# A graph attention layer and a two-of-eight expert layer on one core: where the routing weights come from, and where ScalarE makes the residual rows

## The reference

```python
x = x + gnn(layernorm(x))            # gnn: attention over the edges, then
                                     # (out - mean) * rsqrt(var + eps) * gamma + beta, mean and var over the nodes,
                                     # and + its own input (the residual)
x = x + ffn(layernorm(x))

# in ffn, for the rows xt of its input:
logits  = xt @ Wr + br
probs   = softmax(logits)
top_p, top_idx = top_k(probs, 2)
weights = top_p / top_p.sum(-1)      # of the two chosen experts
xn      = (xt - mean) * rsqrt(var + eps)
out     = sum over the two of  weight * (gelu((xn * ln_g + ln_b) @ W1 + b1) @ W2 + b2)
```

## Time and profile before

| | |
|---|---|
| median of three executions | 1970.54 us |
| the profiled execution's own time | 1971.19 us |
| its span, which all stretches below count | 1969.4 us |
| PE busy / granted clock over the span | 88% / 0.94 |
| DVE, ACT, POOL busy | 73%, 55%, 62% |
| share of PE, DVE and POOL in the chain that ended last | 49%, 16%, 14% |

### The profile page before, as it was taken

How to read it: one execution, slowest core, us unless ns; L and a number is a source line. 1 busy time by engine, 2 the same in 40 slices (tenths; PEclk the granted TensorE clock), 3 DMA queues, 4 the chain that set the end, 5 groups by cost and what they waited for, 6 DMA issues and landing times.

```text
span 1969.4 us, 36324 instructions
## 1 busy us (share of the span) xinstructions
PE 1734.1 (88%) x10852; PEld 1222.6 (62%) x10852; DVE 1438.8 (73%) x3115; ACT 1080.1 (55%) x2380; POOL 1219.4 (62%) x1150
## 2 busy tenths in 40 slices
PE   7769899999999989989898987644999999999997
PEld 5535555555555545555455554543889898989996
DVE  7777777868788777787877878798666666666664
ACT  5656666656666665666666663662444434343443
POOL 1277777777777777777777774102366565556553
PEclk9979999989999999999999989775999999999999
DMA  5554446455465455654546452387132333333322
GB/s 169 167 151 129 136 140 164 129 142 157 138 167 142 134 147 140 165 141 134 148 139 165 121 136 65 117 290 208 31 53 47 53 47 53 48 52 49 51 42 34
DMA packets 142680, 233.52 MB, mean 119 GB/s; under 512 B 31127, under 2 KB 107553, under 8 KB 141313
## 3 DMA queue, kind: packets, MB, share of 16 engines
q0 software_dynamic: 62800, 147.54, 31.4%
q1 hardware_dynamic: 69765, 81.13, 13.5%
q10 hardware_dynamic: 9932, 2.52, 0.7%
HBM read 188.81 MB, written 43.15 MB: 118 GB/s over the span
## 4 chain that ended last, share of the span: by engine, by line
PE 49%; DVE 16%; POOL 14%; issue 10%; DMA 7%; ACT 2%; DVEq 1%; ACTq 0%; POOLq 0%; SPq 0%
PE bank L1940 14%; POOL gather_ring L1061 14%; PE bank L1957 14%; PE bank L1185 8%; PE bank L1150 6%; DVE acc L1079 4%; DMA gather_ring<-node_table,src_slot 3%; DVE gather_ring L1106 2%; DMA w_stage<-in_L_ffn_W 2%; PE bank L930 2%; PE bank L1161 1%; PE bank L1921 1%; PE bank L678 1%; DVE w_lo L953 1%; ACT r_ring L1330 1%
## 5 line engine op out<-in xcount | busy, mean ns | idle before, releaser
L1061 POOL DMA_INDIRECT gather_ring<-node_table,src_slot x879 | 846.0, 962 | 268.0 <-issue 254.3
L1185 PE MATMUL bank<-gather_ring,onehot 128*128 128x264 f32 x1758 | 479.0, 409 | 91.4 <-DVE acc L1079 87.6
L1079 DVE TENSOR_TENSOR acc<-acc,bank 128x264 f32 x879 | 377.2, 429 | 194.6 <-DVE acc L1079 103.4
L1185 PEld LDWEIGHTS bank<-gather_ring,onehot 128*128 128x128 f32 x1758 | 315.8, 192 | 242.0 <-DVE acc L1079 189.8
L1150 PE MATMUL bank<-ones 128*128 128x512 bf16 x1760 | 421.9, 395 | 0.0
L2024 POOL DMA_INDIRECT out_rows<-y,token_idx x105 | 201.4, 1918 | 221.7 <-DMA out_rows<-y,token_idx 151.1
L1150 PEld LDWEIGHTS bank<-ones 128*128 128x128 bf16 x1760 | 170.3, 101 | 200.8 <-issue 32.6
L1992 ACT ACTIVATE hid<-bank,cols 128x256 f32<-128x256 f32 (+1 forms) x448 | 210.3, 551 | 141.5 <-PE bank L1940 138.6
L1940 PE MATMUL bank<-xe,w_hi 128*128 128x256 f16 (+1 forms) x1792 | 284.7, 267 | 0.9 <-ACT hid L1992 0.5
L1957 PE MATMUL bank<-w,hid_hi 128*128 x1680 | 278.3, 273 | 0.1
L1206 ACT ACTIVATE onehot<-iota_free,neg_dst 128x128 f32<-128x128 f32 x880 | 267.3, 386 | 0.0
(11 more groups left out here) (286 smaller groups left out, 2023.3 us busy)
## 6 DMA issues: line engine op xcount, KB each, us to landing
w_stage<-in_L_ffn_W SPq DMA_DIRECT2D x16, 1024.0 KB, 5.5
dst_row<-dst_rows SPq DMA_DIRECT2D x110, 128.0 KB
gather_ring<-node_table,src_slot POOLq DMA_INDIRECT x879, 2.8
w_split<-w_out SPq DMA_DIRECT2D x32, 256.0 KB, 3.0
w<-w_split SPq DMA_DIRECT2D x8, 1024.0 KB, 13.0
node_table<-acc SPq DMA_DIRECT2D x24, 264.0 KB
xt<-in_x SPq DMA_DIRECT2D x24, 256.0 KB, 3.0
r_ring<-in_x SPq DMA_DIRECT2D x6, 896.0 KB, 10.6
```

Of the source, the lines that this page charges most:

```text
L1061: e.indirect_dma_start(out=gather_ring[:, b % GB, j, :], out_offset=None, in_=node_table, in_offset=bass.IndirectOffsetOnAxis(ap=src_slot[ ...
L1079: e.tensor_tensor(a, a, bank[AGG[s % len(AGG)]][:, 0:ROW].rearrange("p (a c) -> p a c", a=1), ALU.add).then_inc(added, 1)
L1185: e.matmul(bank[AGG[s % len(AGG)]][:, 0:ROW], onehot[:, b % OHB, j, :], gather_ring[:, b % GB, j, :], start=True, stop=True).then_inc(summ ...
```

## The change

In the norm, ACT takes a root of ones first of all, makes the copies of all chunks without residual rows between them, and makes all 24 residual rows behind the root of the variance. In stage 3 the two additions and multiplications of all logits that stood at the head of the routing move into the waits for the roots of the second half, the softmax is gone, the two largest are found among the logits themselves, and ACT takes exp of one number per token, their difference, behind its first two groups of rows. FAR_BELOW is -1e38. At the head of the experts' stage DVE splits the first input before vector_columns and columns, and PE turns the first tiles before it waits for the experts.

```diff
--- before.py
+++ after.py
@@ -1418,14 +1418,12 @@
                                  chunk_bank(c, k)[:, 0:len(at) * P].rearrange("p (n m) -> p n m", m=P), ACT.Copy
                                  ).then_inc(chunk_kept, 1)
 
+            e.activation(sd_col, ones[:, 0:KD], ACT.Sqrt)
             for c in range(CHUNKS):
                 keep(c)
-                for n in range(2 * (c - 2), 2 * (c - 1)):
-                    if 0 <= n:
-                        scalar_resid(e, n)
             e.wait_ge(var_known, 1)
             e.activation(sd_col, var_col, ACT.Sqrt, bias=eps[:, :]).then_inc(sd_made, 1)
-            for n in range(2 * (CHUNKS - 2), RESID_AHEAD):
+            for n in range(RESID_AHEAD):
                 scalar_resid(e, n)
 
         def pool_iotas(e):
@@ -1523,7 +1521,13 @@
                 if n == 6 * NG:
                     gains(0)
             variances(1)
+            pr = prob[:, :, :]
+            e.wait_ge(logits_kept, NT)
+            vector_order.of(e.tensor_tensor(pr, pr, logits[:, :, :], ALU.add))
             second(1)
+            e.wait_ge(vector_order.sem, vector_order.n)
+            vector_order.of(e.tensor_tensor(pr, pr, rs1[:, :].rearrange("p (n a) -> p n a", a=1).broadcast_to([P, NT, NE]),
+                                            ALU.mult))
             gains(1)
 
         def vector_route(e):
@@ -1543,20 +1547,13 @@
             pr, IE = prob[:, :, :], iota_e[:, :, :]
             peak, at, w0, w1 = (top[:, i, :] for i in range(4))
             by_tile = "p n e -> p e n"
-            e.wait_ge(logits_kept, NT)
             e.wait_ge(vector_order.sem, vector_order.n)
-            tt(pr, pr, logits[:, :, :], ALU.add)
-            tt(pr, pr, per_tile(rs1[:, :]), ALU.mult)
             tt(pr, pr, per_expert(br_row[:, :]), ALU.add)
-            reduce_e(peak, pr, ALU.max)
-            e.tensor_tensor(pr, pr, per_tile(peak), ALU.subtract).then_inc(logits_shifted, 1)
-            e.wait_ge(exps_made, 1)
-            reduce_e(peak, pr, ALU.add)
-            chain(e, e.reciprocal(peak, peak))
-            tt(pr, pr, per_tile(peak), ALU.mult)
             for c, best in enumerate((w0, w1)):
                 F3 = first[:, c, :, :]
                 reduce_e(best, pr, ALU.max)
+                if c:
+                    e.tensor_tensor(peak, w1, w0, ALU.subtract).then_inc(logits_shifted, 1)
                 tt(Q, pr, per_tile(best), ALU.is_equal)
                 tt(Q, Q, IE, ALU.mult)
                 reduce_e(at, Q, ALU.min)
@@ -1565,14 +1562,15 @@
                         meta[:, :, FIRST_COL - D:FIRST_COL - D + 1].rearrange("p n a -> p (n a)"), at, float(NE), ALU.add))
                 tt(F3, IE, per_tile(at), ALU.is_equal)
                 if c == 0:
-                    chain(e, e.scalar_tensor_tensor(pr, F3, -2.0, pr, ALU.mult, ALU.add))
+                    chain(e, e.scalar_tensor_tensor(pr, F3, FAR_BELOW, pr, ALU.mult, ALU.add))
             tt(chosen[:, :, :], first[:, 0, :, :], first[:, 1, :, :], ALU.add)
             e.tensor_tensor(chosen[:, :, :], chosen[:, :, :], per_tile(valid[:, :]), ALU.mult).then_inc(chosen_made, 1)
 
-            tt(peak, w0, w1, ALU.add)
-            chain(e, e.reciprocal(peak, peak))
-            vector_order.of(e.tensor_tensor(meta[:, :, 0:1].rearrange("p n a -> p (n a)"), w0, peak, ALU.mult))
-            e.tensor_tensor(meta[:, :, 1:2].rearrange("p n a -> p (n a)"), w1, peak, ALU.mult).then_inc(meta_made, 1)
+            e.wait_ge(exps_made, 1)
+            chain(e, e.tensor_single_scalar(w0, peak, 1.0, ALU.add))
+            chain(e, e.reciprocal(w1, w0))
+            vector_order.of(e.tensor_copy(meta[:, :, 0:1].rearrange("p n a -> p (n a)"), w1))
+            e.tensor_tensor(meta[:, :, 1:2].rearrange("p n a -> p (n a)"), peak, w1, ALU.mult).then_inc(meta_made, 1)
 
             def by_expert(psum):
                 return bank[psum][:, 0:NT * NE].rearrange("p (e n) -> p n e", n=NT)
@@ -1670,7 +1668,6 @@
             tt(slot_e[:, 0, :], slot_e[:, 0, :], slot_e[:, 1, :], ALU.add)
             chain(e, e.tensor_single_scalar(expert_of_slot_f[:, :], slot_e[:, 0, :], float(LAST_E), ALU.min))
             e.tensor_copy(expert_of_slot[:, :], expert_of_slot_f[:, :]).then_inc(experts_known, 1)
-            vector_columns(e)
 
         def tensor_stage3(e):
             e.wait_ge(chunk_kept, KD * CHUNKS)
@@ -1726,16 +1723,18 @@
                                         scale=gain[:, n:n + 1])
                 made.then_inc(rows_made, 1)
 
-            assert GROUPS == RB + 2 and RESID_AHEAD + LATE_AT > RB * NG > 2 * (CHUNKS - 2)
+            assert GROUPS == RB + 2 and RESID_AHEAD + LATE_AT > RB * NG
             for g in range(5):
                 keep_logits(g)
             sds(0)
             keep_logits(5)
             keep_logits(6)
             sds(1)
+            for g in range(2):
+                rows(g)
             e.wait_ge(logits_shifted, 1)
-            e.activation(prob[:, :, :], prob[:, :, :], ACT.Exp).then_inc(exps_made, 1)
-            for g in range(GROUPS):
+            e.activation(top[:, 0, :], top[:, 0, :], ACT.Exp).then_inc(exps_made, 1)
+            for g in range(2, GROUPS):
                 rows(g)
             e.wait_ge(meta_made, 1)
             e.dma_start(x_rows[0:(NT - 1) * P, D:XROW].rearrange("(n p) c -> p n c", p=P), meta[:, 0:NT - 1, :]
@@ -1895,9 +1894,11 @@
             e.wait_ge(experts_known, 1)
             for i in range(2):
                 e.wait_ge(rows_stored[i], (STORED[0], ROWS_STORED)[i])
+            split_input(0)
+            vector_columns(e)
+            e.wait_ge(vector_order.sem, vector_order.n)
             for s in range(2):
                 columns(s)
-            split_input(0)
             for s in range(FS + 1):
                 if s + 1 < FS:
                     split_input(s + 1)
@@ -1959,8 +1960,10 @@
                                             start=(c == 0 and n == 0), stop=(c == KH - 1 and n == 2))
                 made.then_inc(y_done, 1)
 
+            for i in range(2):
+                e.wait_ge(rows_stored[i], (STORED[0], ROWS_STORED)[i])
+            turn(0)
             e.wait_ge(experts_known, 1)
-            turn(0)
             for s in range(FS + 1):
                 if s + 1 < FS:
                     turn(s + 1)
```

## The result

After, the kernel takes **1964.62 us** (median of ten executions, 1962.73 to 1967.84), against 1971.48 for the kernel before on the same chip (ten, 1967.12 to 1975.20). The ratio is 0.9967 with an interval of 0.9958 to 0.9976: 6.5 us faster, between 4.7 and 8.3. I had forecast 10.6 less, 1960.0 within 1957.5 to 1964.2. The direction was right, the size was not. (A ratio here is taken over the executions of both kernels and is not exactly the quotient of the two medians, which differ by 6.9 us.)

The account below looks back on a forecast made before the run. The prediction saw the kernel bound by the engine-to-engine path from the last edge to the first hidden matmul, with DMA transfers beside it. Savings of 6.0 + 4.45 + 0.15 = 10.6 us gave 1960.0, range 1957.5 to 1964.2.

Parts of the forecast that it names:

- The wait for the root: Norm: DVE no longer waits for ACT's root behind the variance; 3.1 us saved.
- the late logits: Start of x1: ACT copies tile 0's logits at 1266.7, not 1264.3; cost nothing, up to 1 us if PE were fast.
- The pace: Norm: without residual rows between the copies DVE sets the pace, its statistics ending 2.9 us earlier.
- loses 1.0 there, once: Norm: DVE waits 1.0 us at chunk 3, because the root and table load delay ACT's first copy.
- The table load: Norm: taken as 1.28 us; by the skill's 2.66 the norm's loss would be 2.4 and the sum 9.2.
- The routing: Stage 3: softmax operations gone, additions and products moved into waits; 4.45 us saved, bounds 4.0 and 4.65.
- Part 3: Experts' head: gathers wait for meta, starting 2.4 us earlier; the fourth tile lands faster, keeping almost all of 4.45.
- The head: Experts' head: splitting the first input ahead of the columns gains at most 0.16 us; 0.15 taken.
- meta holds the experts' start: Rival: meta doesn't move, gathers start at 1363.5 or later; 6.2 to 8.5 saved, 1962.0 to 1964.4; chance 0.24.
- an early rise of the clock: Rival, x1: PE's clock already up for the first tiles, another 2 us gone, 1958.0; chance 0.08.
- a lasting low one: Rival, x1: PE's clock stays down, 0.47 us more per tile; with 40 tiles 18.8 lost, 1978.8; chance 0.03.

Follow-up runs that it names:

- e8: Changed kernel with meta's large store issued behind the fourth group of rows instead of the last; 2312.20 us, ratio 0.9979 to the kernel before.
- e1: Changed kernel, but SP waits for the store of meta before issuing the four late loads of second weights; 1964.37 us, ratio 0.9956 to the kernel before.
- e2: Changed kernel with the root of ones and its table load ahead of ACT's wait for the edges; 1963.38 us, ratio 0.9942 to the kernel before.
- e12: Changed kernel with the edits of e8 and e2, and b2_all loaded by ACT behind the first slot's gelus; 1957.65 us, ratio 0.9921 to the kernel before.
- e6: e1 with the load of b2_all moved behind ACT's copy of the second slot's rows; 2313.72 us, ratio 0.9968 to the kernel before.
- e10: Changed kernel with the experts' head as before: vector_columns and columns ahead of the first split; 1963.84 us, ratio 0.9956 to the kernel before.
- e7: e6 with the late weight loads waiting for the fourth tile instead of meta; 2312.72 us, ratio 0.9981 to the kernel before.
- e9: Changed kernel with the edits of e7 and e2 together; 2305.21 us, ratio 0.9962 to the kernel before.
- e11: Changed kernel with the edits of e8 and e2, and b2_all loaded by SP behind the fourth tile's landing; 1960.79 us, ratio 0.9938 to the kernel before.
- e4: Changed kernel with the norm of the kernel before; 1971.24 us, ratio 0.9984 to the kernel before.

## Why the prediction was wrong

**The norm: right in its mechanism.** The wait for the root was worth 3.20 (predicted 3.1) and the late logits nothing (x1 starts as long behind the reciprocal as before). The pace gave 2.26 instead of 2.9. The step "loses 1.0 there, once" was right for the load itself: with the clock up DVE waits 0.99 once, and a is 15.88 (e8), where my terms sum to 16.0. It rested on PE at 1.15 per chunk, which is PE at the full clock; in after the clock fell for some 3 us behind PE's wait, and a is 16.74. That term I had at nothing. It varies from run to run: with the load in the norm a is 15.88 (e8) to 17.78 (e1), and with the load moved away 14.79 (e2) to 15.80 (e12). What decides whether the clock falls, no run shows; the wait alone does not, since it stayed up in e8 and fell in e12.

**The table load** is 1.28 in the norm (1241.94), and the root of ones starts at 1243.24, 0.02 behind it; at 1316.10 the same 1.28, with exp 0.02 behind. The Trainium skill (ScalarE: Activation LUTs, What ACT_TABLE_LOAD costs) adds about 1.38 for a drain; no such time passes around these two. The loss of nearly 2 in the norm comes close to the 2.4 that I worked out by that figure, but only 1.1 of it is the load, as e8 shows, and the rest is PE's clock.

**The routing: right.** 4.54 in place of 4.45.

**Part 3 failed**, in one sentence: "so I take off what they idled, about 0.8 (bounds nothing and 2.5): meta is there at about 1362.7". Measured by the first matmul of x1, meta landed 1.8 later, outside both bounds. I took the landing as the old one less some idle time of the engines, as if meta moved with its issue. But its last packets get through only when the late weights do, in the kernel before as in after: they ended 0.65 and 0.95 behind the weights' last packet, and with the weights held back (e1) meta landed 12 us earlier. What remained to be counted was packets and not bytes: meta is 0.1 MB, but 6250 packets; beside the rows it moved about one for each of theirs, and what was left moved 8 to 13 in a microsecond beside the 8 KB packets. Why the weights themselves ended 1.2 later in after, counted from x1, and 0.1 to 2.4 later over the four kernels with the new routing and this order, is not shown. In numbers, the first gather was to come 2.4 earlier than before and came 0.8 later by x1's clock (5.15 lost behind token_idx against 4.54 - 0.17 + 0.02 won ahead of it). The other half of part 3 was right: the fourth tile lost its 5.2 and took 2.9, because b2_all was out of the way; e6 against e1 shows it by itself. From token_idx to the first hidden matmul the path lost 2.45, of which I had forecast nothing.

**The head: under-counted**, 0.37 for my "at most 0.16": I had set turn(1)'s end as the bound, and in the earlier trace rows those ends are modelled; hidden(0) starts 0.88 behind turn(1)'s start in after, not 1.09.

**The sum.** 10.6 predicted, 8.1 in the path: -0.64 pace, +0.10 root, -0.17 x1, +0.09 routing, +0.02 list, -2.60 from token_idx to the first hidden matmul, +0.68 experts. The last of these is within what the same code does: over the kernels without the late gelu j goes from 592.1 (e10) to 593.7 (e8). The rival "meta holds the experts' start" had the right mechanism, with 1962.0 to 1964.4 against 1964.62. Its account of the fourth tile was wrong, its bound on meta ("doesn't move at all") too mild. That its upper end came so near the time is partly luck: the fourth tile's 2.3, which it did not have, is set off by the norm's 0.6 and the first gather's 0.8, which it did not have either. That rival had 0.24 from me, on the argument that ACT issues earlier; the earlier issue bought nothing. Of the other rivals, x1 showed neither an early rise of the clock nor a lasting low one: it took 40.38 for 40.21.

**What stays open**: why ACT sees the first hidden half 2 us late when it has just issued b2_all (e6, e7, e9; not in e11, where SP issues it, nor in e12, where ACT does so behind the gelus; both differ in the early store of meta as well); what makes PE's clock fall; and what became of the difference between the path's 8.1 and the whole time's 6.5. Larger pieces for meta, which would cut its packets, were not tried.

## What to carry to other kernels

Where two DMA queues are busy, count packets and not bytes: in this kernel a store in pieces of 16 bytes advanced by about one piece for each 1 KB packet of the other queue, and its last pieces landed when that queue's run of large packets was over. So issue such a store where the other queue's packets are small, or where it is empty, and ask what comes behind. Before taking time off a chain, list every other condition of the step at its end and when each is met; one that came 2 us before the last can eat all but 2 us of the gain. And a table load belongs where the engine is idle in any case; ahead of a loop that feeds PE it cost about its own length here. A path read from one execution carries PE's clock in it, so compare the same stretch in several kernels before a difference of 1 us is given a cause.

## What the runs showed that I had not expected

- **Packet for packet.** Beside rows of 1 KB meta moved 251 packets in a microsecond for 251 of the rows (e12), beside next to none over 1500 (before). Issued 2.5 us earlier it landed 1.8 later; issued among the rows (e8) it landed 14 earlier than in after.
- **PE's clock doesn't follow from the pause ahead of it.** In the norm a pause of 3.80 was followed by 0.72 in the mean of 4 us (after), one of 3.68 by 1.00 (e8), one of 2.09 by 0.58 (e12), and one of 1.44 by 1.00 (e2). Column a is 0.7 to 1.9 longer with such a fall than in e8 (with the load) or e2 (without).
- **x1 varies by 3 us with the same code, and the clock is what varies.** Column d goes from 37.8 to 41.2 over kernels that don't differ there. In e7, e8, e9 and e12 the clock is 1.00 from 20 to 28 us behind the first matmul, and d is 37.8 to 38.5. In before and after it is 0.79 there and d 40.2 and 40.4; in e4 and e11 it is 0.62 and 0.61 and d 41.2. That outweighs most of what is asked of one edit, so single paths are to be read by column and not by their sum.
- **The same program took 1973 us on one chip and 2316 on another**, all of the difference in the edges, whose gathers are indirect. The stages behind the edges agreed.
